# A Mamba-2 block with a ternary feed-forward: decay and product rows spread over the partitions by DMA from DRAM instead of by TensorE

## What is computed

```
proj = rmsnorm(x) @ in_proj_w              # z (2048), xBC (2048 + 2*8*64), dt (32)
xBC  = silu(depthwise_conv4(xBC) + conv_b) # x: 32 heads of 64; B, C: 8 groups of 64
dt   = softplus(dt_raw + dt_bias);  dA = exp(-dt * exp(A_log))      # (8, 512, 32)
h_t  = dA_t * h_(t-1) + dt_t * x_t (outer) B_t                      # per head, scan over 512 tokens
y_t  = h_t . C_t + D * x_t
g    = grouped_rmsnorm(y * silu(z)) * gate_norm_w;   x = x + layernorm(x) + g @ out_proj_w
x    = x + ffn(x)
```

## Time and profile before

| | |
|---|---|
| median of three runs | 1291.31 us (1288.37, 1291.31, 1291.34) |
| the profiled execution | 1288.33 us; span from first to last instruction 1286.5 us |
| PE / DVE busy | 1097.4 us (85%) / 1121.1 us (87%) |
| ACT / POOL busy | 973.6 us (76%) / 887.3 us (69%) |
| mean granted TensorE clock | 0.975 of full |
| DMA | 25.44 MB, mean 20 GB/s |
| first decay scan / last decay scan starts | 123.2 us / 1137.0 us |

### The profile page before, as it was taken

How to read it: one execution, slowest core, us unless ns; L and a number is a source line. 1 busy time by engine, 2 the same in 40 slices (tenths; PEclk the granted TensorE clock), 3 DMA queues, 4 the chain that set the end, 5 groups by cost and what they waited for, 6 DMA issues and landing times.

```text
span 1286.5 us, 29886 instructions
## 1 busy us (share of the span) xinstructions
PE 1097.4 (85%) x8970; PEld 726.5 (56%) x8970; DVE 1121.1 (87%) x1967; ACT 973.6 (76%) x2798; POOL 887.3 (69%) x600
## 2 busy tenths in 40 slices
PE   0524788999899989998999899989999999987786
PEld 0513566666566656665666566656666666653565
DVE  8788899999789988998999889988999989857995
ACT  2556788888688878887888888878888888852453
POOL 6560367878587867786778778776878788894321
PEclk9998899999899999999999999999999999997999
DMA  5500000000000000000000000000000000100301
GB/s 150 181 0 0 10 2 2 1 2 2 28 2 2 2 28 2 2 2 28 2 2 2 28 2 2 2 27 2 2 2 10 10 2 2 34 26 27 107 25 33
DMA packets 28803, 25.44 MB, mean 20 GB/s; under 512 B 12112, under 2 KB 22992, under 8 KB 28368
## 3 DMA queue, kind: packets, MB, share of 16 engines
q1 hardware_dynamic: 24400, 21.18, 5.4%
q10 hardware_dynamic: 4224, 2.10, 0.5%
HBM read 14.88 MB, written 8.39 MB: 18 GB/s over the span
## 4 chain that ended last, share of the span: by engine, by line
PE 39%; DVE 25%; issue 16%; ACT 12%; POOL 4%; ACTq 1%; DMA 1%; DVEq 1%; POOLq 0%; SPq 0%
DVE conv L1077 8%; PE bank L1441 5%; PE bank L1458 5%; ACT xw L760 5%; DVE lm L1066 4%; PE bank L1464 4%; PE bank L1385 4%; ACT conv L768 3%; PE bank L1401 3%; PE bank L1496 3%; PE bank L1387 3%; PE bank L1386 3%; PE bank L1417 2%; PE bank L1473 2%; DVE cdec L1107 2%
## 5 line engine op out<-in xcount | busy, mean ns | idle before, releaser
L1077 DVE SCALAR_TENSOR_TENSOR conv<-bank,cw,conv 128x511 f32<-128x511 f32 (+2 forms) x576 | 410.1, 741 | 32.6 <-ACT conv L768 30.2
L1066 DVE TENSOR_TENSOR_SCAN lm<-bank,ident 128x512 f32<-128x512 f32 x256 | 298.5, 1208 | 63.8 <-PE bank L1401 51.6
L615 POOL TENSOR_TENSOR lm<-lm,cbs 128x1024 f32<-128x1024 f32 x128 | 303.3, 2369 | 57.0 <-ACT xw L760 56.4
L798 ACT ACTIVATE xdt<-bank,dt_all 128x64 f32<-128x64 f32 x1024 | 222.6, 332 | 0.0
L601 POOL TENSOR_TENSOR gated<-gated,gate 128x512 f32<-128x512 f32 x128 | 164.2, 1283 | 68.9 <-DVE gated L1116 61.1
L760 ACT ACTIVATE xw<-xdt,lm 128x64 f32<-128x64 f32 x768 | 196.3, 339 | 11.7 <-issue 11.7
L621 POOL TENSOR_TENSOR ssum<-ssum,sq 128x512 f32<-128x512 f32 x96 | 123.2, 1284 | 90.9 <-ACT sq L812 88.3
L1385 PE MATMUL bank<-xn_hi,w_hi 128*128 (+1 forms) x320 | 153.2, 479 | 27.9 <-DVE conv L1077 26.0
L607 POOL TENSOR_TENSOR gated<-gated,rbs 128x512 f32<-128x512 f32 x128 | 164.9, 1289 | 1.3 <-ACT rbs L861 1.3
L1441 PE MATMUL bank<-gated,w_out 128*128 128x512 f32 x256 | 151.9, 677 | 4.9 <-POOL gated L607 3.1
L1458 PEld LDWEIGHTS bank<-lm,xdt 128*64 128x64 f32 x2048 | 110.7, 138 | 80.2 <-issue 79.5
(11 more groups left out here) (183 smaller groups left out, 1832.9 us busy)
## 6 DMA issues: line engine op xcount, KB each, us to landing
lm<-in_L_attn_in_proj_w SPq DMA_DIRECT2D x1, 2048.0 KB, 9.8
xn_scratch<-chan SPq DMA_DIRECT2D x4, 512.0 KB, 4.8
r_stage<-residual_scratch SPq DMA_DIRECT2D x8, 256.0 KB, 3.2
x_scratch<-r_stage SPq DMA_DIRECT2D x8, 256.0 KB, 2.3
cbs<-x_scratch SPq DMA_DIRECT2D x8, 256.0 KB, 2.9
gated<-x_scratch SPq DMA_DIRECT2D x1, 2048.0 KB, 8.0
out_tokens<-gated ACTq DMA_DIRECT2D x8, 256.0 KB, 2.3
xn_stage<-xn_scratch SPq DMA_DIRECT2D x7, 256.0 KB, 2.9
```

Source lines behind the costliest of these rows:

```text
L615: gp.tensor_tensor(lm[:, mr, :, :], lm[:, mr, :, :], cbs[:, :, :], ALU.mult).then_inc(m_done, 1)
L798: act.activation(xdt[:, r, at:at + HP], misc_of("xt", n)[:, at:at + HP], ACT.Copy, scale=dt_h).then_inc(xdt_done, 1)
L1066: V.tensor_tensor_scan(lm[:, m % R, a, :], bc_bank[(3 * m + a) % 2][:, :], ident4[:, :], 0.0, ALU.mult, ALU.add).then_inc(scanned, 1)
L1077: V.scalar_tensor_tensor(out=conv[:, ci % 4, shift:S], in0=tile_bank(b, n, t)[:, 0:S - shift], scalar=cw[:, q, t, KW - 1 - shift:KW - shif ...
```

## The change

1. `spread` is no longer three PSUM banks written by PE but a ring in SBUF, `spread` (128 x 4 x 3 x 512 f32), one place per slot r. Two DRAM tensors hold the rows in f32, one row per head. For every slot SP issues three DMAs: one puts both dA rows on all 128 partitions, two put a product row on 64 partitions each. They wait for `cdec` of four slots before.
2. The scans, `pend` and `cdec` read `spread` in SBUF instead of PSUM. Their sizes are the same.
3. The bf16 splits, `sel`, `da_parts` and `pr_parts` go. One batch of rows at a time is transposed, copied to SBUF, scanned and stored; batch 0 before the first slot, batches 1 to 7 ahead of slots 1, 2 and 3 (`EARLY_ROWS`).
4. With banks 2 and 3 free, z has bank 3 to itself, conv tiles alternate on 0 and 1 alone, and y alternates between 6 and 2 (PE now waits for `skipped` of two pairs before).
5. SP's list is written by slots; the residual's store, wait and load stand at slot 2 of each batch.

```diff
-        proj_bank, bc_bank, misc_bank, y_bank, out_bank = bank[0:2], bank[2:4], bank[4:6], bank[6], bank[7]
+        proj_bank, z_bank, misc_bank, y_bank, out_bank = bank[0:2], bank[3], bank[4:6], (bank[6], bank[2]), bank[7]
...
+EARLY_ROWS = {1: (1, 2), 2: (3, 4), 3: (5, 6, 7)}
+        spread = sb("spread", [P, R, 3, S])
+        da_dram = nc.dram_tensor("decay_scratch", (H, NB * S), F32, kind="Internal").ap()
+        pr_dram = nc.dram_tensor("product_scratch", (H, NB * S), F32, kind="Internal").ap()
...
+            def store_rows(i):
+                sp.wait_ge(rows_ready, i + 1)
+                sp.dma_start(da_dram[:, S * i:S * i + S], da_stage[i % 2]).then_inc(rows_stored[i % 2], 16)
+                sp.dma_start(pr_dram[:, S * i:S * i + S], pr_stage[i % 2]).then_inc(rows_stored[i % 2], 16)
+            def spread_rows(b, m):
+                q, r = divmod(m, R)
+                tok = bass.ds(b * S, S)
+                after(sp, cdec_done, SLOTS, b, m - R)
+                head = 8 * q + r
+                sp.dma_start(spread[:, r, 0:2, :], da_dram[head:head + 5:4, tok].unsqueeze(0).broadcast_to([P, 2, S])).then_inc(spread_loaded[r], 16)
+                for a in range(2):
+                    sp.dma_start(spread[HP * a:HP * a + HP, r, 2, :],
+                                 pr_dram[head + 4 * a:head + 4 * a + 1, tok].broadcast_to([HP, S])).then_inc(spread_loaded[r], 16)
...
+            def rows(i):        # DVE
+                dve.wait_ge(da_copied, i + 1)
+                if i >= 2:
+                    dve.wait_ge(rows_stored[i % 2], 32 * (i // 2))
+                for c in range(CH):
+                    tok = slice(P * c, P * c + P)
+                    V.tensor_tensor_scan(pr_stage[i % 2][:, tok], da_stage[i % 2][:, tok], zeros[:, :], 1.0,
+                                         ALU.mult, ALU.add).then_inc(pr_scan, 1)
...
+                    after(dve, spread_loaded[m % R], 48 * UNITS, bb, 48 * (m // R) + 47)
                     for a in range(2):
-                        after(dve, bc_ready, 3 * SLOTS, bb, 3 * m + a)
-                        V.tensor_tensor_scan(lm[:, m % R, a, :], bc_bank[(3 * m + a) % 2][:, :], ident4[:, :], 0.0,
+                        V.tensor_tensor_scan(lm[:, m % R, a, :], spread[:, m % R, a, :], ident4[:, :], 0.0,
                                              ALU.mult, ALU.add).then_inc(scanned, 1)
...
-                    V.tensor_tensor(cdec[:, m % R, :], bc_bank[(3 * m + 2) % 2][:, :], chan[:, chan_of(m // R, 1), :],
+                    V.tensor_tensor(cdec[:, m % R, :], spread[:, m % R, 2, :], chan[:, chan_of(m // R, 1), :],
                                     ALU.mult).then_inc(cdec_done, 1)
...
-                if ssd is not None:
-                    spread(*ssd, 2)
...
-                    after(pe, skipped, SLOTS, bb, m - 1)
+                    after(pe, skipped, SLOTS, bb, m - 2)
```

More of the change, by code:

```diff
@@ L511, in _ @@
-            batch(0)
-            with sp.Fori(1, NB - 1) as b:
-                batch(b)
-            batch(NB - 1)
+                if n == 2 and not (isinstance(b, int) and b == 0):
+                    residual_turn(b)
+                spread_rows(b, n)
+            store_rows(0)
+            sp.wait_ge(rows_stored[0], 32)
+            for n in range(R):
+                slot(0, n)
+            for i in range(1, NB):
+                store_rows(i)
+            for k in range(2):
+                sp.wait_ge(rows_stored[k], 32 * NB // 2)
@@ L516, in _ @@
+            for n in range(R, SLOTS):
+                slot(0, n)
+            for n in range(SLOTS):
+                slot(1, n)
+            with sp.Fori(2, NB - 1) as b:
+                for n in range(SLOTS):
+                    slot(b, n)
+            for n in range(SLOTS):
+                slot(NB - 1, n)
+            residual_turn(NB)
             sp.wait_ge(silu_done, NB * NCONV)
@@ L787, in slot @@
                 ssd = back(b, n, LAG_SSD)
+                if isinstance(b, int) and (b, n) == (0, LAG_SUM):
+                    for k in range(2):
+                        act.wait_ge(rows_stored[k], 32 * NB // 2)
                 if ssd is not None:
@@ L885, in step @@
                                   fres[:, bass.ds((i - 2) * CH, CH), :]).then_inc(f_stored, 16)
-            slot(0, 0)
-            for i in range(NB):
-                da_rows(i)
-                if i == 0:
-                    pr_copies(None, 3)
-            act.wait_ge(pr_rest, len(PR_ORDER))
-            for n in range(1, SLOTS):
+            for n in range(SLOTS):
+                for i in EARLY_ROWS.get(n, ()):
+                    rows(i)
                 slot(0, n)
@@ L1225, in step @@
                     result()
-            slot(0, 0)
-            left(1, 3)
-            for n in range(1, SLOTS):
+            for n in range(SLOTS):
+                for i in EARLY_ROWS.get(n, ()):
+                    rows(i)
                 slot(0, n)
@@ L1307, in _, with rows @@
             pe.wait_ge(dt_raw, 2)
-            for i in range(NB):
+            def rows(i):
                 if i >= 2:
-                    pe.wait_ge(pr_scan, CH * (i - 1))
+                    pe.wait_ge(da_copied, i - 1)
                 for c in range(CH):
@@ L1313, in _ @@
                     last = TR(bank[2 + i % 2][0:H, P * c:P * c + P], wk[4][:, at:at + H], ident)
[L1314 to L1316 removed]
+                last.then_inc(da_t, 1)
+            rows(0)
             def misc_free(b, n, kind, k=0):
@@ L1519, in slot @@
                     last.then_inc(xo_ready, 1)
-                if back(b, n + 1, LAG_SSD) is not None:
-                    for k in range(2):
-                        spread(*back(b, n + 1, LAG_SSD), k)
             def step(i, par, k):
```

220 lines of the change are left out of this document (56 added, 164 removed).

## The result

The changed kernel takes 1448.67 us (median of 4 runs, 1444.99 to 1451.94) against 1290.04 for the kernel before beside it: ratio 1.123, 95% interval 1.120 to 1.126, so 158.6 us slower. Its profiled span is 1447.5 us.

What follows compares the result with a forecast made beforehand. DVE and POOL were taken to exclude each other on SBUF, giving 9.7 us per slot instead of 7.97. 1288.3 us + 220 (slots) - 8 (first slots) - 14 (preamble) = 1486, as median 1489 us; range 1370 to 1620.

Steps and rivals of the forecast that it cites:

- signs in the profile: Scans: least 1.15 to 1.2 us, mean near 2, maximum above 3; taps unchanged; DVE above 90% busy; DMA near 80 GB/s.
- Bounds by hand ... mean 9.4: Pipeline slots: DVE and POOL alternating in list order take 9.67 or 8.45 us by slot kind, mean 9.4; 9.7 with waits.
- Own length of scan and cdec: left unchanged: Pipeline: reading SBUF instead of PSUM leaves their own lengths; the skill page's estimate of 25 us less is not taken.
- I take 3 us visible, -14: Preamble: DVE passes and a POOL wait go; memsets and 3 us of visible row stores come; -14 us, ends -18 and -3.
- First slots -8: First few slots: no gating and normalising on POOL, about 8 turns less of 1.0 us, -8 us.
- The end "does not change": After the last scan: the end keeps its length, no term in the sum.
- Second y bank, loads: Pipeline: y's 5.6 us wait goes unseen under late DVE; loads hidden by three slots' lead; rival that loads bind, 1616, chance 0.06.
- PE under the cover of DVE: Pipeline: PE works 6.3 of 9.7 us, so its 1.2 us per slot saved is worth nothing under DVE.
- PE's clock: Rival, pipeline: a less busy PE falls to the low clock, 10.2 us per slot passing DVE's 9.4; 1590 us, chance 0.04.
- the few DVE instructions with both tensors in SBUF: Trace reading, quantisation and preamble: these, unlike scans, cdec and taps before the change, are held up by POOL multiplications, whole instructions at a time.
- between two waiting lists they alternate: DVE and POOL: a DVE instruction with two SBUF tensors and a POOL multiplication exclude each other and take turns.
- PE loses the spreading ... the gain would be worth 0.39 us per slot: Pipeline: 384 matmuls of 0.39 us go; without exclusion the gain would be the 0.39 us per slot of DVE's spreading wait.

Runs made afterwards that it cites:

- e1: The changed kernel with the scans' identity operand in PSUM bank 2 and one y bank: 1331.8 us, ratio 1.033 to the kernel before.
- e3: The changed kernel with POOL's four slot instructions cut to 64 columns, the rest of those products left out: 1259.0 us, ratio 0.975.
- e5: The changed kernel with SP issuing the preamble's row stores ahead of the spread loads of the first slots: 1432.6 us, ratio 1.113.
- e2: The changed kernel with one y bank instead of two, identity left in SBUF: 1444.5 us, ratio 1.119.
- e4: The changed kernel with one more 512 KB DMA per slot into a spare buffer: 1470.0 us, ratio 1.139.
- e8: The kernel before, plus 768 KB per slot broadcast from DRAM into an unused spare buffer: 1288.1 us, ratio 1.001.
- e12: e5 plus PE's projections ahead of the transposes in the second slot of four: 1416.0 us, ratio 1.098.
- e7: The changed kernel with one y bank and three extra unread PE matmuls per slot: 1442.7 us, ratio 1.118.
- e6: The changed kernel with identity in PSUM, one y bank, stores ordered ahead of loads, and pend copied by ACT: 1277.5 us, ratio 0.990.
- e11: The kernel before with only PE's projections put ahead of the transposes in the second slot of four: 1288.8 us, ratio 1.000.
- e9: e6 plus PE's projections ahead of the transposes in the second slot of four: 1254.3 us, ratio 0.975.

## Why the prediction was right, and where its sizes were off

The forecast was 1489 us, the result 1449, +159 where +198 was expected. The direction, the mechanism and its signs in the profile came as described: least scan 1.19 us, mean 1.74, maximum 3.3, taps unchanged, DVE above 90%, the waits for PE gone, about 90 GB/s. e1 (take one operand out of SBUF) and e3 (take POOL's time away) each remove most of it.

The sum came closer than its terms. The slots, with the first few, were put 54 us too high (+212 against 158), the preamble 11 us and the end 6 us too low, and these errors partly cancel: 1486 - 54 + 11 + 6 = 1449, the profiled execution.

**"Bounds by hand ... mean 9.4"** was 0.5 us too much. Measured per slot: scans 2 x (1740 - 1206) ns = 1.07 us, `pend` 588 - 154 = 0.43, `cdec` 905 - 682 = 0.22: 1.73 us of exclusion where 9.4 - 7.13 = 2.27 were counted. 7.13 + 1.73 = 8.86, and DVE's busy share in the windows gives the same, 692.5 / 720 x 9.21 = 8.86. The order of the turns was right; the lengths in it were too long. In the slot shown, scan, L602 and scan take 3.29 us where 3.52 was counted, since POOL holds the access for about 1.05 us, not 1.22; taps and states take 622.31 to 626.74 = 4.43 us where six times 0.68 and 0.57 made 4.65; the rest is as counted, 1.50. Together 0.45, and 9.67 becomes 9.22. The remaining waits, taken as 0.3, are 9.21 - 8.86 = 0.35. By kind of slot (88 slots, from the scans' starts) the counted 8.45 was 8.06, and the counted 9.67 was 9.22 and 9.39; the second slot of four took 10.57, since DVE's waits for the convolution stand there.

**Own length of scan and cdec: left unchanged.** Right: 1191 and 675 ns at least, against 1190 and 674. The Trainium skill, VectorE: DVE Perf Modes, section "The TRN2 errata", gives 120 cycles of fixed cost from PSUM and 58 from SBUF at 0.96 GHz; the 65 ns less that I estimate from this are seen in neither. The measurement decides.

**Preamble: "I take 3 us visible, -14".** Measured -3.3, and the first scan at 119.9 us instead of "near 109". The passes saved are worth at least 18.3 us (e5), where 12 + 5.7 - 1 = 16.7 were counted. What failed is the pricing of the stores by their landing time of 2.3 us: I had noted that SP issues twelve loads before the second store, and gave this no price. It costs 15 us, once.

**First slots -8** can't be separated in the trace. **The end "does not change"**: +6.4 us, and 148.6 with the identity in PSUM. So it goes with the scans' operand. It stands in the few slots behind the last scan: from its start to the start of the last `gated` it takes 24.6 us (1291.6 to 1316.2), against 16.9 before and 18.1 in e1. The last two scans (4.87 us together, 2.34 before) and `cdec` (1.64) still wait for POOL there, and the drain behind them comes later.

**Second y bank, loads: worth nothing or hidden.** e2, e4 and e8 agree. No run takes z's own bank back, so its worth stays untested. **PE under the cover of DVE** was right only in part: in e12 PE's order alone was worth 17 us beside the whole exclusion. **PE's clock** did fall, from 0.975 to 0.888, as that rival said. It doesn't carry the loss, since the exclusion of 1.73 us per slot does; whether it costs a few us, e7 leaves open.

**Which instructions are held up.** SBUF — State Buffer, "SBUF: two separate sides", of the Trainium skill, names two kinds of DVE instruction that exclude GpSimd: those with two SBUF inputs, and those in a mode that uses both ports for one tensor, which a copy or a `tensor_scalar` can enter. The runs agree for scans and `cdec`, and `pend`, a copy with one SBUF input, was held up as well (mean 588 ns, 154 undisturbed), as the prediction counted it. But its reading of the trace, "the few DVE instructions with both tensors in SBUF", was too narrow. The same stretch before the change held an instruction with one tensor, which fared worst:

```profile
1155.11 5.42 DVE L1252 TENSOR_SCALAR conv<-conv,xn_stage 128x512 f32<-128x512 f32 x1
1160.56 0.43 DVE L1253 TENSOR_SCALAR conv<-conv 128x512 f32<-128x512 f32 x1
```

```profile
1155.30 1.28 POOL L601 TENSOR_TENSOR gated<-gated,gate 128x512 f32<-128x512 f32 x1
...
1158.96 1.28 POOL L607 TENSOR_TENSOR gated<-gated,rbs 128x512 f32<-128x512 f32 x1
```

Four POOL multiplications ran in a row from 1155.30 to 1160.24 before L1252 got through. So "between two waiting lists they alternate" did not hold there. In the slots it did, as the timeline of the result shows, and the hand count rests on that; no row ahead of the prediction had it for scans. (A slip of reading: L962 takes 1.22 us six times, not four.)

**"PE loses the spreading ... the gain would be worth 0.39 us per slot"** was not tested by the changed kernel, and in e3 and e6 it turned out wrong. Without spreading, and with only `cdec` still held up (980 - 682 ns = 0.30 us per slot), e6's slot was 8.02 us; e3's, with nearly nothing held up, was 7.85, where 7.4 had been counted. The 44 us that the list of waits puts down to the spreading were the end of the turn of four, in which several things come late; the next in line, projections behind `cb`, its copy and the transposes, took its place. A gain on the slots needed both, the rows from DRAM and PE's order: the first with the preamble is worth 1.0%, the second alone nothing (e11), together 2.5%.

## What to carry to other kernels

Before a tensor moves from PSUM to SBUF to relieve PE, look at what else DVE's reading instruction reads, and at POOL's load: with all its tensors in SBUF each such instruction and each of POOL's multiplications run one after the other. Putting the constant operand into a PSUM bank took 0.90 us per slot of the loss back, but not all: of the versions that compute everything, the first with a slot clearly shorter than before is the one that changes PE's order too (e9, 7.80 us against 7.97). A wait that disappears from the list is worth only its distance to the next late thing at the same place, and a queue filled with early loads must be priced for whatever stands behind them.
